# Fourth attention of a four-layer kernel: the values of four heads in three pieces instead of two, and a fifth key tile masked on VectorE instead of TensorE

## The reference

```python
def _L3_xattn_ref(q, k, v, mask, Wq, bq, Wk, bk, Wv, bv, Wo, bo):
    Q = _split(q @ Wq.T + bq)          # q = layernorm(x), k = v = ctx_1024
    K = _split(k @ Wk.T + bk)
    V = _split(v @ Wv.T + bv)
    scores = jnp.einsum('bhqd,bhkd->bhqk', Q, K) / np.sqrt(HEAD_DIM)
    scores = jnp.where(mask == 0, jnp.float32(-1000000000.0), scores)
    attn = jax.nn.softmax(scores, axis=-1)
    out = jnp.einsum('bhqk,bhkd->bhqd', attn, V)
    return out.transpose(0, 2, 1, 3).reshape(...) @ Wo.T + bo
x = x + _L3_xattn_ref(_layernorm(x), ctx_1024, ctx_1024, mask_1x1xSxS2_ik0, ...)
```

## Time and profile before

| what | us |
|---|---|
| median of 3 runs | 2109.28 |
| lowest and highest | 2107.88, 2111.71 |
| the profiled execution | 2111.81 |
| its span in the trace | 2110.0 |
| fourth attention, first score to last value matmul | 1676.8 to 2082.3 |
| TensorE busy in the span | 1899.7 (90%) |
| VectorE busy | 1334.4 (63%) |
| ScalarE busy | 1297.4 (61%) |
| GpSimd busy | 309.7 (15%) |

### The profile page before, as it was taken

How to read it: one execution, slowest core, us unless ns; L and a number is a source line. 1 busy time by engine, 2 the same in 40 slices (tenths; PEclk the granted TensorE clock), 3 DMA queues, 4 the chain that set the end, 5 groups by cost and what they waited for, 6 DMA issues and landing times. The chain is left out here.

```text
span 2110.0 us, 43468 instructions
## 1 busy us (share of the span) xinstructions
PE 1899.7 (90%) x16932; PEld 1336.2 (63%) x16935; DVE 1334.4 (63%) x3286; ACT 1297.4 (61%) x2097; POOL 309.7 (15%) x475
## 2 busy tenths in 40 slices
PE   6999999967868659999999999999995799999997
PEld 4777777735634637777777777777774456666553
DVE  7888888877455244555555555555555877777773
ACT  5999999955356125555555555555564466666664
POOL 4000000000122110000000000000000445555552
PEclk9999999977877679999999999999997799999998
DMA  7211111102260510000000000000000621111110
GB/s 239 58 43 47 42 47 43 42 16 77 48 187 18 150 36 2 1 1 1 1 2 1 1 1 2 1 1 1 1 2 1 210 57 42 47 43 47 47 37 17
DMA packets 55307, 87.69 MB, mean 42 GB/s; under 512 B 9881, under 2 KB 31437, under 8 KB 55105
## 3 DMA queue, kind: packets, MB, share of 16 engines
q1 hardware_dynamic: 54593, 83.87, 13.5%
q0 software_dynamic: 512, 1.05, 0.2%
HBM read 66.93 MB, written 17.96 MB: 40 GB/s over the span
## 5 line engine op out<-in xcount | busy, mean ns | idle before, releaser
L2528 ACT ACTIVATE a_prT<-bank 128x512 f32<-128x512 f32 (+1 forms) x448 | 232.8, 565 | 328.2 <-PE bank L2437 328.0
L1226 DVE CUSTOM_DVE_ANT_0 a_attn_junk<-wide,a_mask 128x801 f32<-128x801 f32 (+1 forms) x256 | 246.1, 990 | 92.0 <-PE wide L1023 91.2
L2583 DVE CUSTOM_DVE_ANT_0 a_sc<-wide,a_zeros 128x1024 f32<-128x1024 f32 (+1 forms) x256 | 243.1, 987 | 87.3 <-PE wide L2423 87.3
L1149 ACT ACTIVATE a_attn_prT<-bank 128x512 f32<-128x512 f32 (+1 forms) x378 | 196.9, 567 | 106.6 <-PE bank L1043 103.5
L1554 DVE CUSTOM_DVE_ANT_0 a_attn_sc<-wide,a_mask 128x801 f32<-128x801 f32 (+1 forms) x256 | 252.9, 988 | 12.3 <-PE wide L1401 10.6
L1417 PE MATMUL bank<-ident,a_attn_sc 128*128 128x128 f32 x1664 | 244.8, 276 | 14.9 <-ACT a_attn_prT L1511 13.8
L1417 PEld LDWEIGHTS bank<-ident,a_attn_sc 128*128 128x128 f32 x1664 | 199.0, 142 | 62.3 <-issue 42.3
L2437 PE MATMUL bank<-ident,a_sc 128*128 128x128 f32 x1664 | 231.3, 277 | 1.5 <-ACT a_prT L2528 1.5
L2437 PEld LDWEIGHTS bank<-ident,a_sc 128*128 128x128 f32 x1664 | 185.1, 140 | 54.4 <-issue 28.1
L1517 ACT ACTIVATE a_attn_sc<-a_attn_sc,a_attn_nmx 128x1601 f32<-128x1601 f32 x128 | 209.6, 1637 | 3.0 <-DVE a_attn_nmx L1560 3.0
L2489 PEld LDWEIGHTS bank<-a_prT,a_vt 128*64 128x64 f32 x3328 | 180.3, 137 | 48.4 <-issue 47.0
(11 more groups left out here) (476 smaller groups left out, 3089.8 us busy)
## 6 DMA issues: line engine op xcount, KB each, us to landing
a_ks<-a_k_parts SPq DMA_DIRECT2D x384, 75.0 KB
a_k_parts<-a_proj_kp SPq DMA_DIRECT2D x18, 416.0 KB, 4.9
a_qx<-a_q_stack SPq DMA_DIRECT2D x384, 12.0 KB
moe_w1b<-in_e_w SPq DMA_DIRECT2D x15, 256.0 KB, 3.0
ctxT<-in_ctxT SPq DMA_DIRECT2D x4, 832.0 KB, 6.5
a_ctxn<-in_ctxn SPq DMA_DIRECT2D x4, 832.0 KB, 7.1
a_k_parts<-a_last_slot SPq DMA_DIRECT2D x6, 416.0 KB, 4.1
m_q_stack<-m_proj_qp SPq DMA_DIRECT2D x9, 256.0 KB, 3.5
```

Of the source, the lines that this page charges most:

```text
L1149: act.activation(probs(u)[0:keys, kt:kt + m, :], bank_of(s, f"W{g}")[0:keys, 0:m * S].rearrange("p (t q) -> p t q", q=S), ACT.Exp).then_in ...
L1226: dve.tensor_tensor_reduce(junk[:, n % 2, 0:w], S_WIDE[n % 2][:, 0:w], mask(qt, at, w), 1.0, LOWEST, ALU.add, ALU.max, mx[:, p % 2, qt, e, ...
L2528: copy = lambda out, src: act.activation(out, src, ACT.Copy)
L2583: dve.tensor_tensor_reduce(sc[:, s % 2, h, at:at + w], S_WIDE[h][:, 0:w], zeros[:, 0:w], 1.0, LOWEST, ALU.add, ALU.max, mx[:, s % 2, h, p: ...
```

## The change

`CAPPED_TILES` goes from 4 to 5. Tile 4, the first of group W2, gets no mask matmul any more; its exponentials are capped by a second instruction of VectorE in each step (256 columns, after maximum 2). The set-up gets one short instruction more in each of two places (`cap` has five tiles, `maskT` eight). `CHUNKS` has three pieces, 20, 16 and 16 matmuls in steps A, B and C, so that copying, turning and normalising the sums move from B to C, a batch's end from C to D, and the stage has one step more. `values(s)` moves behind `turned_group(s, 0)` and `score_piece(s, 0)`. ScalarE now waits before each group's exponentials for the pieces of values that read that part of the buffer, where it waited once per unit for all of them.

```diff
-CAPPED_TILES = 4
+CAPPED_TILES = 5
...
-    CHUNKS = [(0, 7), (7, KT)]
-    CAPPED = CAPPED_TILES // 2
+    CHUNKS = [(0, 5), (5, 9), (9, KT)]
...
-    LAST = UNITS + TURN + 4
+    LAST = UNITS + TURN + 5
...
         def batch_end(s):
-            b = (s - 21) // 16
-            return b if s >= 21 and (s - 21) % 16 == 0 and b < B else None
+            b = (s - 22) // 16
+            return b if s >= 22 and (s - 22) % 16 == 0 and b < B else None
+
+        def chunks_before(kt):
+            return sum(first < kt for first, last in CHUNKS)
...
-                    if g >= CAPPED:
+                    if kt + j >= CAPPED_TILES:
                         pe.matmul(out, core.identb[:, 0:keys], mask_rows(kt + j), start=True, stop=False)
...
-                pe.wait_ge(capped, 4 * q + 4)
+                pe.wait_ge(capped, 2 * (4 * q + 4))
...
-                if last == KT:
-                    ins.then_inc(pv_done, 1)
+                ins.then_inc(pv_done, 1)
...
             for s in range(LAST):
                 if s == 1:
                     count_valid()
-                values(s)
                 turned_group(s, 0)
                 score_piece(s, 0)
+                values(s)
                 turned_group(s, 1)
...
                 if g == 0:
                     act.wait_ge(setup, 5 if u >= PRT - 1 else 4)
-                    if u >= PRT:
-                        act.wait_ge(pv_done, (u - PRT) // 4 + 1)
+                if u >= PRT:
+                    act.wait_ge(pv_done, len(CHUNKS) * ((u - PRT) // 4) + chunks_before(kt + m))
...
-                        act.wait_ge(pv_done, q + 1)
+                        act.wait_ge(pv_done, len(CHUNKS) * (q + 1))
...
-                dve.wait_ge(exp_done, NG * u + 1)
-                dve.tensor_tensor(probs(u)[:, 0:2, :], probs(u)[:, 0:2, :], cap[:, 0:2, :], ALU.min).then_inc(capped, 1)
+                dve.wait_ge(exp_done, NG * u + g + 1)
+                at, end = (0, 2) if g == 0 else (4, 5)
+                dve.tensor_tensor(probs(u)[:, at:end, :], probs(u)[:, at:end, :], cap[:, at:end, :], ALU.min).then_inc(capped, 1)
...
-                for i in range(2):
-                    dve.tensor_tensor(cap[:, 2 * i:2 * i + 2, :], cap[:, 2 * i:2 * i + 2, :],
-                                      alone[:, i:i + 1, :].broadcast_to([P, 2, S]), ALU.max).then_inc(flagged, 1)
+                for at, end, i in ((0, 2, 0), (2, 4, 1), (4, 5, 0)):
+                    dve.tensor_tensor(cap[:, at:end, :], cap[:, at:end, :],
+                                      alone[:, i:i + 1, :].broadcast_to([P, end - at, S]), ALU.max).then_inc(flagged, 1)
...
                 maximum(s, 1)
-                cap_masked(s)
+                cap_masked(s, 0)
                 maximum(s, 2)
+                cap_masked(s, 2)
                 normalise(s)
                 maximum(s, 3)
```

More of the change, by code:

```diff
@@ L1040, in turned_group @@
                     out = bank[0:keys, j * S:(j + 1) * S]
-                    if g >= CAPPED:
+                    if kt + j >= CAPPED_TILES:
                         pe.matmul(out, core.identb[:, 0:keys], mask_rows(kt + j), start=True, stop=False)
                     ins = pe.matmul(out, ks[0:MAX_ROW + 6, u % RING, at:at + keys], qx[0:MAX_ROW + 6, u % RING, :],
-                                    start=g < CAPPED, stop=True)
+                                    start=kt + j < CAPPED_TILES, stop=True)
                 ins.then_inc(turned, 1)
@@ L1232, in maximum, with cap_masked @@
                     dve.tensor_reduce(nmx[:, p % 2, :, :], mx[:, p % 2, :, :, :], X, ALU.max, negate=True).then_inc(max_ready, 1)
-            def cap_masked(s):
+            def cap_masked(s, g):
                 u = s - TURN
@@ L1237, in cap_masked @@
                     return
-                if u == 0:
-                    dve.wait_ge(flagged, 4)
-                dve.wait_ge(exp_done, NG * u + 1)
-                dve.tensor_tensor(probs(u)[:, 0:2, :], probs(u)[:, 0:2, :], cap[:, 0:2, :], ALU.min).then_inc(capped, 1)
+                if u == 0 and g == 0:
+                    dve.wait_ge(flagged, 6)
+                dve.wait_ge(exp_done, NG * u + g + 1)
+                at, end = (0, 2) if g == 0 else (4, 5)
+                dve.tensor_tensor(probs(u)[:, at:end, :], probs(u)[:, at:end, :], cap[:, at:end, :], ALU.min).then_inc(capped, 1)
             def flag_all_masked():
@@ L1854, in masked_head_layer @@
             if replaced:
-                for at, given in ((0, CAP), (2, 1.0)):
-                    mask_work[1].append(lambda dve, at=at, given=given: dve.tensor_scalar(
-                        cap[:, at:at + 2, :], seenT[:, at:at + 2, :], 0.0, given, ALU.not_equal, ALU.mult))
+                for at, end, given in ((0, 2, CAP), (2, 4, 1.0), (4, 5, CAP)):
+                    mask_work[1].append(lambda dve, at=at, end=end, given=given: dve.tensor_scalar(
+                        cap[:, at:end, :], seenT[:, at:end, :], 0.0, given, ALU.not_equal, ALU.mult))
             layernorm_stage(core, ln, core.x, core.xn, core.xnT, loads=loads, ahead=() if replaced else ahead,
```

## The result

The changed kernel takes 2121.04 us (median of 6 runs, 2115.67 to 2125.01). The kernel before, run beside it, has a median of 2110.91 over 6 runs. The ratio is 1.0053 with a 95% interval of 1.0042 to 1.0064: slower, by 10.1 us in the medians. The direction of the forecast was right. Its size, +6.2 us, was too small, and the measured time lies 1 us above the range. The profiled execution took 2121.11 us with a span of 2119.3, against 2111.81 and 2110.0 in before.

What follows compares the result with a forecast made beforehand. No engine is full; the chain from one quad's values to the next bounds it, 24.28 us becoming 24.75. 14 x 0.47 = 6.6, + 1.4 start, - 0.75 batches, - 1.05 end = +6.2 us: 2115.5 from the median, range 2105 to 2120.

Steps and rivals of the forecast that it cites:

- C to the reduction (5.04 + 2.66): Values of C to VectorE's maximum 2, 5.04 us, then from there to the reduction of the maxima, 2.66 us.
- reduction to the values (4.26 + 0.28): End of the quad: GpSimd's path from the reduction to the next values of A, 4.26 us, plus 0.28 for the collision.
- VectorE decides from A to B and from B to C: Between values, VectorE is late, not TensorE: 6.47 and 6.04 us, the saved mask matmul bringing only 0.11.
- The copy holds the turning in C (0.59): In C, TensorE waits 0.59 us for ScalarE's copy of the sums; without the wait maximum 2 comes 0.57 earlier.
- Second cap and normalising on the path in C (2.66): From maximum 2 of C to the reduction, the new cap and the normalising both count: 2.66 us.
- The collision: In D the new cap falls inside GpSimd's weighing; of three bounds (nothing, 0.28, 0.42) 0.28 us a quad was taken.
- third bound: In D VectorE stands until GpSimd's instruction is through, 0.42 us a quad; as rival +8.2 us, 2117.5, chance 0.15.
- The start, +1.4: Before quad 0: one cap more in each of steps 3 to 5, +1.05, set-up +0.1, collision +0.28; together +1.4 us.
- The batches, -0.75: Three batches' ends move from C to the end of D, 0.35 us each becoming some 0.1: -0.75 us.
- The end, -1.05: Quad 14 to the last values: 20.7 us instead of 21.74, the last values partly beside exponentials: -1.05 us.
- Ahead of and behind the stage, nothing: Projections, loads and the other layers outside the stage: no change, 0 us.
- only the copy wrong: Rival in C: the collision stays, the wait for the copy goes; 24.18 us a quad, 2108.7, no change, chance 0.10.

Runs made afterwards that it cites:

- e1: The changed kernel with the fifth key tile's mask back on TensorE (four capped tiles, three pieces of values kept); 2111.34 us, ratio 1.0005.
- e9: e8 with four capped tiles instead of five; 2102.32 us, ratio 0.9965.
- e8: The changed kernel with values first in the step, the 256-column cap ahead of maximum 2 in every step, and the sums turned one score piece later; 2108.36 us, ratio 0.9994.
- e10: e9 with key tiles 2 and 3 moved to the second piece and the wait for GpSimd's weighing only from there on; 2093.67 us, ratio 0.9924.
- e11: e10 with five capped tiles instead of four; 2096.66 us, ratio 0.9936.
- e4: The changed kernel with the turning of the sums moved behind the next turned group and score piece; 2113.85 us, ratio 1.0019.
- e5: The changed kernel with GpSimd's two-input L1203 replaced by a one-input minimum against a constant, leaving out the mask of tiles 2 and 3; 2117.82 us.
- e3: The changed kernel with the 256-column cap put ahead of maximum 2 in step D alone; 2116.09 us, ratio 1.0030.
- e2: The changed kernel with values back in two pieces at the start of steps A and B, five capped tiles kept; 2151.25 us, ratio 1.0200.

## Why the prediction came out as it did

Link by link, measured on the starts of the values and the reduction, in quad 5, which is like the others:

| link | predicted | measured |
|---|---|---|
| A to B | 6.47 | 6.47 |
| B to C | 6.04 | 6.09 |
| C to the reduction (5.04 + 2.66) | 7.70 | 7.67 |
| reduction to the values (4.26 + 0.28) | 4.54 | 4.64 |
| quad | 24.75 | 24.87 |

Quad 6, whose rows are shown here, is the one that isn't like the others. B to C takes 6.34 us in it. ScalarE starts its exponentials of B 0.28 us later behind W1 than in quad 5. The same quad has 0.12 to 0.26 more from B to C in every kernel with three pieces; why is open. S0 and the values of B, then the values of C:

```profile
1872.25 0.50 PE L1025 MATMUL wide<-a_ks,a_qx 72*128 72x512 bf16 x2 [0.23 <-DVE a_attn_mx L1227]
1872.68 1.92 PE L1075 MATMUL bank<-a_attn_prT,a_vs 128*9 128x256 f32 x32
...
1879.02 1.92 PE L1075 MATMUL bank<-a_attn_prT,a_vs 128*9 128x256 f32 x32
```

- **VectorE decides from A to B and from B to C, so that the saved mask matmul brings 0.11 us:** right in size (6.48 against 6.59 in e1), and e9 against e8 and e10 against e11 show that the fifth tile gives the quad nothing. S0 waits 0.23 us for VectorE ahead of the values of B, where I had said 0.4.
- **The copy holds the turning in C (0.59):** right. The turning starts 3.76 us behind the values of C where the sum had 3.78, though the row shows a wait of only 0.39. e4 took it away and gained the 0.57 there that the prediction named, before a new collision took 0.22 back.
- **Second cap and normalising on the path in C (2.66):** right, 2.65.
- **The collision:** this is the step that failed, in its choice among three bounds. I took "GpSimd is held for the cap's columns", 0.28, as nearest to the row in which L1202 took 1.57 us. That row has a cap that starts first. Here GpSimd starts first, and VectorE is held until it is through, with its own columns still to do (0.28 us). That is the third bound, the rival with 24.47 + 0.42 = 24.89 us a quad, and 24.88 was measured. The match is in part luck: it took a full cap of 0.42 and 0.14 to the values behind L1202, and measured are 0.28 and 0.25. Against it I had set that no cap in the trace is ever longer than another. That was no evidence, since the only cap of before that started inside L1202 (2073.11) did so 0.10 us ahead of its end. The Trainium skill ("SBUF — State Buffer", section "Who interferes with whom") has the rule that whoever starts first holds the port for its whole length. For L1203, with two inputs, after agrees: 0.92 us instead of 0.42.
- **Where it collides:** I looked at D alone. It happens in A (0.65 us) and B (0.64) as well, hidden there: in e5, where no cap is held, A to B and B to C take the same 6.48 and 6.09. (The 0.05 that B to C is over the sum is no matter of the cap; e1, without it, has it too, 6.20 against 6.15.) It also happens in the steps ahead of quad 0, where both caps are met:

```profile
1704.61 1.16 POOL L1203 TENSOR_TENSOR a_attn_prT<-a_attn_prT,a_cap 128x512 f32<-128x512 f32 x1
1705.13 0.91 DVE L1243 TENSOR_TENSOR a_attn_prT<-a_attn_prT,a_cap 128x256 f32<-128x256 f32 x1
1708.37 1.16 POOL L1203 TENSOR_TENSOR a_attn_prT<-a_attn_prT,a_cap 128x512 f32<-128x512 f32 x1
1708.70 1.38 DVE L1243 TENSOR_TENSOR a_attn_prT<-a_attn_prT,a_cap 128x512 f32<-128x512 f32 x1
```

- **The start, +1.4:** too small by 1.2, by the same failed step. The sum had one collision at 0.28. Three caps are held, the two above by 0.50 and 0.69 us and the one in D, at 1715.74, by 0.50. With e5, where none is held, the start is 1.25 us shorter and 1.31 over before, near the 1.1 that the sum gives without collisions. e1, without the fifth tile, has the start of before (36.95).
- **The batches, -0.75:** right in kind and a little low: the three ends cost 0.04 together instead of 1.0. What stood in for it in the total is the 0.24 of quad 6, which no part of the sum knew.
- **The end, -1.05:** too good by 0.7. The last 16 matmuls hide less than I worked out by the prices of the steady quads. Which step of it fails wasn't followed further.
- **Ahead of and behind the stage, nothing:** +0.57 and -1.0. In the last feed-forward part of after the first two matmuls of L879 took 0.70 instead of 1.22 us, as at a higher clock. The other kernels' first scores, over 8 us apart with the same code ahead of them, show that a part like +0.57 is not the change's.

Sum: 0.57 + 2.56 + 7.57 - 0.37 - 1.04 = 9.3 us. With 14 x 0.60 for the quads, and the start and the end as measured, the sum would have been 14 x 0.60 - 0.75 + 2.6 - 0.4 = +9.9. The range ended at 2120 since the rival's sum carried only one held cap at the start; and the 3 runs then known had a median 1.6 us below that of the 6. One sum of the prediction has a slip: the rival "only the copy wrong" comes to 14 x -0.10 + 1.4 - 1.8 = -1.8, 2107.5 and not 2108.7, which changes neither its class nor a chance.

## What to carry to other kernels

When two engines' instructions are going to overlap for the first time, price each order of starting by itself: a row in which VectorE starts first says nothing of the case in which GpSimd does. Before work is taken off an engine, look at which chain closes the loop: here the mask matmul was worth nothing, while reading the tiles that GpSimd finishes last in the second piece brought 12 us in six changed lines. And after each edit look for what slides into a neighbour: two of these runs gave back part of their gain, one because a cap moved into L1203 (e4), one because a wait moved onto S0 (e3).

## What the runs showed of the hardware

- A VectorE minimum of two SBUF tiles that starts inside a GpSimd `TENSOR_TENSOR` with two inputs ends behind it by the time of its own columns: 0.28 us for 256 columns (0.42 became 0.92, 0.65 and 0.64; the same 0.28 for all 45 such caps in after), 0.55 for 512 (0.69 became 1.38 and 1.56). One that started only 0.10 us ahead of L1202's end kept its 0.69. A one-input `TENSOR_SCALAR` on VectorE is held too, and ends 0.14 behind with 256 columns (0.29 became 0.78).
- A one-input `TENSOR_SCALAR` on GpSimd held none of the caps that ran inside it (0.69 and 0.42 us, means of 687 and 425 ns in e5).
- With VectorE ahead, it is GpSimd that is stretched, by what is left of VectorE's columns: a cap of 512 columns 0.13 us ahead makes 1.57 of 1.16 us (0.55 less 0.13), and one of 256 columns 0.10 ahead makes 1.34 (0.28 less 0.10; e8).
- In e2, where TensorE waits 1.3 us behind a held cap, the granted clock of whole stretches fell from 1.00 to 0.88, with score pieces of 0.85 instead of 0.50 us, and quads took up to 29.8 us instead of 26.1. Other quads of e2 have the same wait and stayed at 1.00, so the wait alone doesn't decide it. In after, with waits of up to 0.5 us in a quad, the clock stayed at 1.00. What set it off was not tried by itself.
